# Loading the expert numbers of the tiles into TensorE's registers: eight at a time or two at a time

## The chip, the cores and the metric

The kernel runs on one core of one Trainium2 chip. The metric is device time in microseconds (us) of one execution, the median of several runs. Its engines are named as the profile names them: PE (TensorE, with PEld for its weight loads and PEldq for what its sequencer does itself), DVE (VectorE), ACT (ScalarE), POOL (GpSimd) and SP (SyncE).

## The reference, cut to what matters

The program is a chain of four blocks, each added to its input after a layernorm: differential attention (batch 16, 256 tokens, width 128), a two-layer window-attention transformer, a linear state-space recurrence, and a mixture of experts. Only the last is touched:

```python
xt = x.reshape(-1, D)                        # 4096 tokens, D = 128
logits = xt @ router_w.T                     # 8 experts
topk_vals, topk_idx = jax.lax.top_k(logits, 2)
g = jax.nn.sigmoid(topk_vals)
g = g / (g.sum(axis=-1, keepdims=True) + 1e-10)
out = jnp.zeros_like(xt)
for e in range(E):
    ge = jnp.sum(jnp.where(topk_idx == e, g, jnp.zeros_like(g)), axis=-1)
    h = jax.nn.silu(xt @ w_gate[e]) * (xt @ w_up[e])      # width 256
    out = out + ge[:, None] * (h @ w_down[e])
```

Every token takes part in two experts only, so the kernel sorts the tokens by expert and multiplies each with the weights of its own two.

## The kernel before, in words

A stage called `dispatch` has written every token's row (128 numbers, its place and its expert) into a region of DRAM for each of its two experts. `mixture_of_experts` then works through 72 tiles (`SLOTS = 2 * TILES + NE`) of 128 rows, each of one expert. Which expert a tile has is known only on the chip: VectorE counts (`tiles_of_experts`) and writes the expert of each tile into `c["count"]` and the place of its rows into `c["place"]`, both int32 in SBUF, then raises `listed`.

What each engine does with the tiles, in a fixed order written out by hand as Python loops:

- SyncE loads eight places at a time into registers (L1757) and issues one load per tile into a ring of 16 (`xin`, L1763). A slot is used again once TensorE has turned its rows (`x_full`) and VectorE has aimed them (`aimed`).
- TensorE: `turn_x(q)` transposes the rows of tiles 2q and 2q+1 into `psX` (L1918); `gate_up(i)` multiplies tile i with the gate and up weights of its expert, 512 columns, into `psG` (L1925); `turn_h(i)` transposes the hidden values (L1933); `down(i)` multiplies with the down weights, two halves (L1941). The order in iteration i is: `turn_x` for the next pair (even i), `gate_up(i + 1)`, `turn_h(i)`, `down(i - 1)`.
- ScalarE moves the transposed rows out of PSUM (`mx_xT`, L1873), takes silu of the gate half (`mx_sl`, L1880) and moves the turned hidden values (`mx_hT`, L1886).
- VectorE multiplies silu with the up half (`mx_h`, L1847), copies the result out (`mx_y`, L1854), and every eight tiles works out where rows go (`aim`).
- GpSimd scatters the 128 result rows of each tile to DRAM (`mx_results`, L1772).

The weights of all experts lie in SBUF (`m_experts`). The address of a tile's weights is computed from a register of TensorE's sequencer, which `load_experts(n)` (L1901 to L1907) fills: eight values of `c["count"]` per call (`SHARE = 8`), in one TENSOR_LOAD followed by a FUSED_REGOPS and a SEQ_ASSERT for each value, all recorded under L1903. It is called once ahead of the loop and then at i = 4, 12, ..., 60 for the tiles from i + 4 on, between `turn_x` and `gate_up(i + 1)`. Each product has a further FUSED_REGOPS of its own for the address (recorded under L1925 and L1941), and waits for semaphores that don't fit on an instruction are EVENT_SEMAPHORE instructions of the sequencer (L1931 ahead of `turn_h`, L1939 ahead of `down`).

Behind the last tile and its scatter a barrier follows, and then the stage that fetches both results of each token, weighs and adds them, normalises and stores.

Of the kernel before, what the change touches and what calls it, by code (L numbers as in the profile page):

```python
# [1473 lines left out]
NE = 8  # L1474
# [6 lines left out]
SLOTS = 2 * TILES + NE  # L1481
SHARE = 8
# [217 lines left out]
def mixture_of_experts(nc, X, F, out, rows, results, consts, c, w, pay, top, seen):  # L1700
# [7 lines left out]
    with ExitStack() as ctx:  # L1708
# [4 lines left out]
        with ExitStack() as tiles_ctx:  # L1713
# [35 lines left out]
            def x_of(eng, i):  # L1749
                eng.wait_ge(landed[i % RING], 16 * (i // RING + 1))  # L1750

            @block.sync
            def _(sp):
                sp.wait_ge(listed, 1)
                for i in range(SLOTS):
                    if i % SHARE == 0:
                        _, at = nc.values_load_multi_w_load_instructions(  # L1757
                            c["place"][0:1, i:i + SHARE], engines=(mybir.EngineType.SP,), min_val=0,
                            max_val=(NE + 1) * TILES * P - P)
                    if i >= RING:  # L1760
                        sp.wait_ge(x_full, (i - RING) // 2 + 1)
                        sp.wait_ge(aimed, (i - RING) // SHARE + 1)
                    sp.dma_start(xin[:, i % RING, :], rows[bass.ds(at[i % SHARE], P), :])\  # L1763
                      .then_inc(landed[i % RING], 16)
# [133 lines left out]
            @block.tensor  # L1898
            def _(pe):
                chosen = {}  # L1900

                def load_experts(n):
                    _, values = nc.values_load_multi_w_load_instructions(  # L1903
                        c["count"][0:1, n * SHARE:(n + 1) * SHARE], engines=(mybir.EngineType.PE,), min_val=0,
                        max_val=NE - 1)
                    for k, v in enumerate(values):
                        chosen[n * SHARE + k] = v  # L1907

                def of_expert(i, c0, c1):
                    return weights[:, bass.ds(chosen[i], 1), c0:c1].rearrange("p a n -> p (a n)")  # L1910

                def turn_x(q):
                    for i in (2 * q, 2 * q + 1):
                        x_of(pe, i)
                    if q >= 1:
                        pe.wait_ge(xT_ready, q)
                    for a in range(2):
                        ins = pe.transpose(psX[:, a * P:(a + 1) * P], xin[:, (2 * q + a) % RING, 0:D], ident[:, :])  # L1918
                    ins.then_inc(x_full, 1)

                def gate_up(i):
                    pe.wait_ge(xT_ready, i // 2 + 1)
                    if i >= 2:
                        pe.wait_ge(h_ready, i - 1)
                    pe.matmul(psG[:, i % 2, :], xT[:, i // 2 % 2, i % 2, :], of_expert(i, 0, DOWN), start=True, stop=True)\  # L1925
                      .then_inc(g_full, 1)

                def turn_h(i):
                    pe.wait_ge(h_ready, i + 1)
                    if i >= 2:  # L1930
                        pe.wait_ge(hT_ready, i - 1)  # L1931
                    for j in range(J):
                        ins = pe.transpose(psH[:, i % 2, j * P:(j + 1) * P], h[:, i % 2, j * P:(j + 1) * P], ident[:, :])  # L1933
                    ins.then_inc(t_full, 1)

                def down(i):
                    pe.wait_ge(hT_ready, i + 1)
                    if i >= 2:
                        pe.wait_ge(y_ready, i - 1)  # L1939
                    for j in range(J):  # L1940
                        ins = pe.matmul(psY[:, i % 2, 0:D], hT[:, i % 2, j * P:(j + 1) * P],  # L1941
                                        of_expert(i, DOWN + j * D, DOWN + (j + 1) * D), start=(j == 0), stop=(j == J - 1))
                    ins.then_inc(y_full, 1)

                pe.matmul(psC[:, 0:NE], c["ones"][:, :], seen[:, GROUPS, :], start=True, stop=True).then_inc(counted, 1)
                pe.wait_ge(listed, 1)
                load_experts(0)
                turn_x(0)
                gate_up(0)
                for i in range(SLOTS):  # L1950
                    if i % 2 == 0 and i + 2 < SLOTS:
                        turn_x(i // 2 + 1)
                    if i % SHARE == SHARE // 2 and i // SHARE + 1 < SLOTS // SHARE:
                        load_experts(i // SHARE + 1)
                    if i + 1 < SLOTS:
                        gate_up(i + 1)
                    turn_h(i)
                    if i >= 1:
                        down(i - 1)
                down(SLOTS - 1)  # L1960
# [327 lines left out]
```

## Time and profile before

| what | us |
| --- | --- |
| runs, median (lowest to highest of 3) | 2120.12 (2118.52 to 2121.19) |
| the profiled execution, its own time | 2117.38 |
| span of its records | 2115.6 |
| PE busy in the span | 1730.7 (82%) |
| DVE busy | 1544.2 (73%) |
| ACT busy | 1364.1 (64%) |
| POOL busy | 876.9 (41%) |
| mean granted clock of TensorE (share of full speed) | 0.906 |

The profile is of one execution. Times in its rows are counted from the span's start. A row of the timeline merges like instructions in a row; what stands in brackets is how long the engine was idle before and what released it. "issue" is idle time in which the engine waited for nothing that the profile shows, so it is its sequencer that was late. Register and semaphore instructions do not count as busy; they are found under PEldq at their line. A matmul's end is modelled, so that two matmuls in a row can overlap in the rows. The granted clock (PEclk) is 1.00 for 2.4 GHz and 0.50 for 1.2 GHz, or a mean over both.

### The profile page before, as it was taken

The page shows a single profiled execution, that of the slowest core. Times are in us where ns is not written, and L with a number is a line of the kernel's source. Part 1 is how long each engine was busy: PE and PEld are TensorE (multiplying, and loading weights), DVE is VectorE, ACT ScalarE, POOL GpSimd, SP SyncE. Part 2 cuts the span into 40 slices and gives each one's busy share as a digit, 9 for nine tenths or more (in the row PEclk, how much of TensorE's full clock was granted, in tenths as well). Part 3 has the DMA queues.
Part 4 walks back from the last instruction along what each step waited for, and adds up shares of the span by engine and source line. Part 5 has one row for each costly group of instructions (what it writes and reads, how often), then busy time and mean ns, then how long its engine had stood idle before and what let it go on. Part 6 is the DMA issues. An engine that isn't in the chain of part 4 may idle for free. (4 is left out here: it accounts for less than half of the span.)

```text
span 2115.6 us, 39585 instructions
## 1 busy us (share of the span) xinstructions
PE 1730.7 (82%) x12410; PEld 1135.5 (54%) x12410; DVE 1544.2 (73%) x4156; ACT 1364.1 (64%) x4708; POOL 876.9 (41%) x816
## 2 busy tenths in 40 slices
PE   4999999999999937999996868999996836426881
PEld 2555555555555515777774535777773514424550
DVE  3888999898988857999994658999993656513334
ACT  2888888888888835888883226888882262303444
POOL 3555555565555633333321233323231231662444
PEclk9999999999999957999998979999998966558995
DMA  7990000000000000000001100000001000112214
GB/s 208 202 155 2 2 2 2 2 2 2 2 2 2 2 5 6 17 11 16 16 16 24 27 6 11 11 16 17 16 11 33 18 1 1 36 46 66 64 45 128
DMA packets 102527, 65.92 MB, mean 31 GB/s; under 512 B 27698, under 2 KB 93874, under 8 KB 102322
## 3 DMA queue, kind: packets, MB, share of 16 engines
q1 hardware_dynamic: 97970, 54.40, 12.3%
q0 software_dynamic: 4352, 8.99, 1.2%
q8 instruction: 104, 1.70, 0.3%
q14 instruction: 101, 0.83, 0.1%
HBM read 19.50 MB, written 30.24 MB: 24 GB/s over the span
## 5 line engine op out<-in xcount | busy, mean ns | idle before, releaser
L411 ACT ACTIVATE a_E<-a_psS,a_nm 128x128 f32<-128x128 f32 (+1 forms) x1028 | 419.9, 429 | 31.2 <-DVE a_nm L245 28.8
L216 POOL TENSOR_SCALAR a_aT<-a_dT 128x384 f32<-128x384 f32 x256 | 309.8, 1210 | 298.8 <-PE a_psO L529 187.3
L245 DVE TENSOR_REDUCE a_nm<-a_psS 128x2 f32<-128x256 f32 (+1 forms) x514 | 259.9, 546 | 43.8 <-PE a_psS L496 43.2
L492 PE MATMUL a_psS<-a_kT,a_qm 32*128 32x128 f32 (+1 forms) x2064 | 240.6, 351 | 5.7 <-issue 3.7
L270 DVE SCALAR_TENSOR_TENSOR a_d<-a_E,a_cf 128x128 f32<-128x128 f32 (+1 forms) x512 | 219.5, 469 | 27.9 <-DVE a_cf L259 1.4
L411 ACT ACTIVATION_READ_ACCUMULATOR a_E<-a_psS,a_nm 128x1 f32 x1028 | 220.6, 215 | 0.0
L830 POOL TENSOR_TENSOR b0rn<-b0ss,minus_half 128x16 f32<-128x16 f32 x36 | 107.2, 2977 | 224.2 <-DVE b0ss L866 224.2
L830 POOL TENSOR_TENSOR b1rn<-b1ss,minus_half 128x16 f32<-128x16 f32 x36 | 107.2, 2977 | 223.3 <-DVE b1ss L866 223.3
L420 ACT ACTIVATE a_dT<-a_psT 128x384 f32<-128x384 f32 x256 | 127.0, 496 | 73.8 <-PE a_psT L505 71.1
L492 PEld LDWEIGHTS a_psS<-a_kT,a_qm 32*128 32x128 f32 x2064 | 136.6, 186 | 56.1 <-issue 35.7
L505 PE MATMUL a_psT<-ident,a_d 128*128 128x128 f32 x768 | 132.4, 281 | 6.1 <-DVE a_d L270 0.3
L1772 POOL DMA_INDIRECT mx_results<-mx_y,mx_targetu x72 | 68.8, 955 | 106.3 <-DVE mx_y L1854 105.7
L505 PEld LDWEIGHTS a_psT<-ident,a_d 128*128 128x128 f32 x768 | 87.6, 141 | 34.7 <-DVE a_d L270 28.4
L1847 DVE TENSOR_TENSOR mx_h<-mx_psG,mx_sl 128x256 f32<-128x256 f32 x72 | 30.6, 425 | 102.7 <-ACT mx_sl L1880 99.0
L496 PE MATMUL a_psS<-causal,identb 128*128 128x256 bf16 x516 | 101.8, 279 | 0.0
L1925 PE MATMUL mx_psG<-m_experts,mx_xT 128*128 x144 | 83.9, 668 | 18.7 <-issue 18.1
L964 ACT ACTIVATE b0E<-b0psS,b0nm 128x128 f32<-128x128 f32 x260 | 92.0, 377 | 10.0 <-DVE b0nm L894 10.0
L964 ACT ACTIVATE b1E<-b1psS,b1nm 128x128 f32<-128x128 f32 x260 | 92.0, 377 | 8.7 <-DVE b1nm L894 8.7
L1077 PE MATMUL b0psQ<-wqk,b0hT 128*128 128x512 f32 x148 | 81.3, 676 | 16.9 <-DVE b0part L875 12.0
L1077 PE MATMUL b1psQ<-wqk,b1hT 128*128 128x512 f32 x148 | 80.4, 669 | 16.8 <-DVE b1part L875 11.3
L1046 PEld LDWEIGHTS b0psS<-b0kT,b0qm 128*128 128x128 f32 x528 | 72.1, 198 | 18.2 <-issue 16.3
L518 PE MATMUL a_psO<-a_dT,a_vp 128*32 128x256 f32 x516 | 81.2, 393 | 0.6 <-ACT a_dT L420 0.6
(353 smaller groups left out, 4425.7 us busy)
## 6 DMA issues: line engine op xcount, KB each, us to landing
mx_rows<-mx_blank SPq DMA_DIRECT2D x9, 2080.0 KB, 27.9
mx_xin<-mx_rows SPq DMA_DIRECT2D x72, 65.0 KB, 1.9
b0v<-b0v SPq DMA_DIRECT2D x34, 128.0 KB, 2.3
b1v<-b1v SPq DMA_DIRECT2D x34, 128.0 KB, 2.3
F<-mx_results SPq DMA_DIRECT2D x8, 256.0 KB, 5.1
mx_second<-mx_results SPq DMA_DIRECT2D x8, 256.0 KB, 5.6
out_dram<-X SPq DMA_DIRECT2D x8, 256.0 KB, 2.3
f0z<-F SPq DMA_DIRECT2D x9, 128.0 KB
```

The lines of the kernel that those rows point to most:

```text
L216: pool.tensor_scalar(aT[:, s, :], dT[:, s, :], 0.0, None, ALU.max).then_inc(positived.sem, 1)
L245: ins = dve.tensor_reduce(nm[:, s, t, :], psS[:, s, :, (0, P)[t]:(P, 384)[t]], axis=AX.X, op=ALU.max, negate=True)
L270: ins = dve.scalar_tensor_tensor(out=d[:, s, c0:c1], in0=E[:, s, 1, c0:c1], scalar=cf[:, s, t:t + 1], in1=E[:, s, 0, c0:c1], op0=ALU.mult, ...
L411: ins = act.activation(E[:, s, m, c0:c1], psS[:, s, m, c0:c1], ACT.Exp, bias=nm[:, s, t, m:m + 1], accum_out=Z[:, p, h, t, m:m + 1])
L420: act.activation(dT[:, s, :], psT[:, s, 0:384], ACT.Copy).then_inc(evaced.sem, 1)
L492: pe.matmul(psS[:, s, m, c0:c1], qm[rows, p, a, r, t * P:(t + 1) * P], kT[rows, p, a, 0:c1 - c0], start=(t == 0), stop=False)
L496: ins = pe.matmul(diagonal, identb[:, :], causal[:, :].unsqueeze(1).broadcast_to([P, 2, P]), start=False, stop=True)
L505: ins = pe.transpose(psT[:, s, c * P:(c + 1) * P], d[:, s, c * P:(c + 1) * P], ident[:, :])
L830: pool.tensor_tensor(rn[:, t, :], ss[:, t, :], minus_half[:, 0:2 * H], ALU.pow).then_inc(rn_ready.sem, 1)
L964: ins = act.activation(E[:, s, n, :], psS[:, s, n * P:(n + 1) * P], ACT.Exp, bias=nm[:, s, n:n + 1], accum_out=Z[:, s, n:n + 1])
L1077: ins = pe.matmul(psQ[:, n * W:(n + 1) * W], hT[:, p, t * P:(t + 1) * P], wqk[:, n * W:(n + 1) * W], start=True, stop=True)
L1925: pe.matmul(psG[:, i % 2, :], xT[:, i // 2 % 2, i % 2, :], of_expert(i, 0, DOWN), start=True, stop=True)\
```

## The change

`load_experts` takes two values a call instead of eight. The first call, ahead of the loop, is for tiles 0 and 1; then it is called at every even i for tiles i + 2 and i + 3. Its place in the iteration is now behind `gate_up(i + 1)`, ahead of `turn_h(i)`, where it stood between `turn_x` and `gate_up(i + 1)`. Nothing else is changed. TensorE's stream gets 36 TENSOR_LOADs in place of 9, and the same 72 pairs of register instructions. All lines behind L1904 are one lower in the changed kernel between the two edits.

```diff
-                def load_experts(n):
+                def load_experts(i):
                     _, values = nc.values_load_multi_w_load_instructions(
-                        c["count"][0:1, n * SHARE:(n + 1) * SHARE], engines=(mybir.EngineType.PE,), min_val=0,
-                        max_val=NE - 1)
+                        c["count"][0:1, i:i + 2], engines=(mybir.EngineType.PE,), min_val=0, max_val=NE - 1)
                     for k, v in enumerate(values):
-                        chosen[n * SHARE + k] = v
+                        chosen[i + k] = v
...
                 for i in range(SLOTS):
                     if i % 2 == 0 and i + 2 < SLOTS:
                         turn_x(i // 2 + 1)
-                    if i % SHARE == SHARE // 2 and i // SHARE + 1 < SLOTS // SHARE:
-                        load_experts(i // SHARE + 1)
                     if i + 1 < SLOTS:
                         gate_up(i + 1)
+                    if i % 2 == 0 and i + 2 < SLOTS:
+                        load_experts(i + 2)
                     turn_h(i)
                     if i >= 1:
                         down(i - 1)
```

On TensorE, iteration 4 before: the turns of x for tiles 6 and 7, the load for tiles 8 to 15 (`ISA x16` are the eight register pairs), and the gate-and-up product of tile 5.

```order
L1941 MATMUL mx_psY<-m_experts,mx_hT 128x128
L1918 MATMUL mx_psX<-ident,mx_xin 128x128 x2
L1903 TENSOR_LOAD mx_count
L1903 ISA x16
L1925 ISA
L1925 MATMUL mx_psG<-m_experts,mx_xT 128x512
```

The same iteration on TensorE in the changed kernel, up to the first down product of tile 3.

```order
L1940 MATMUL mx_psY<-m_experts,mx_hT 128x128
L1917 MATMUL mx_psX<-ident,mx_xin 128x128 x2
L1924 ISA
L1924 MATMUL mx_psG<-m_experts,mx_xT 128x512
L1903 TENSOR_LOAD mx_count
L1903 ISA x4
L1932 MATMUL mx_psH<-ident,mx_h 128x128 x2
L1940 ISA
L1940 MATMUL mx_psY<-m_experts,mx_hT 128x128
```

The product of tile 5 has moved ahead of the load, the load has four register instructions instead of sixteen, and it stands in front of the turns of h of tile 4. The same piece comes in each even iteration.

## Rows read from the trace of the kernel before

**Rows 1.** The page's head
```profile
span 2115.6 us, 39585 instructions
```

**Rows 2.** Busy time by stretches of the expert tiles (columns in its first line)
```profile
core 0: us, PE busy (x) PEld busy (x) DVE busy (x) ACT busy (x) POOL busy (x), PEclk, DMA share, GB/s
1912.00:2072.00 160.00, 135.29 (x648) 88.22 (x648) 50.47 (x171) 63.62 (x181) 68.78 (x72) 0.89 0.22 61
...
1928.50:1932.00 3.50, 3.41 (x9) 2.24 (x10) 0.45 (x2) 0.77 (x2) 0.00 (x0) 0.53 0.50 128
1932.00:1943.00 11.00, 11.00 (x62) 7.34 (x60) 4.50 (x16) 5.46 (x17) 6.30 (x7) 1.00 0.27 73
1945.80:1958.70 12.90, 12.90 (x70) 8.68 (x71) 4.86 (x18) 6.18 (x19) 6.36 (x7) 1.00 0.23 62
1961.30:1966.00 4.70, 4.70 (x16) 3.03 (x17) 1.12 (x3) 1.43 (x4) 0.96 (x1) 0.64 0.07 20
```

**Rows 3.** Waits of PE, 1912 to 2072 us (total us, times, longest)
```profile
PE mx_psG L1925 <- issue: 18.1, 8, 2.4
PE mx_psX L1918 <- DMA mx_xin<-mx_rows: 10.9, 1, 10.9
```

**Rows 4.** Timeline of PE (start, us, engine, line, op, operands, times)
```profile
1925.82 0.38 PE L1918 MATMUL mx_psX<-ident,mx_xin 128*128 128x128 f32 x2
1928.59 2.07 PE L1925 MATMUL mx_psG<-m_experts,mx_xT 128*128 x2 [2.39 <-issue]
...
1936.57 0.38 PE L1918 MATMUL mx_psX<-ident,mx_xin 128*128 128x128 f32 x2
1936.79 1.02 PE L1925 MATMUL mx_psG<-m_experts,mx_xT 128*128 x2
...
1943.11 0.38 PE L1918 MATMUL mx_psX<-ident,mx_xin 128*128 128x128 f32 x2
1945.79 1.12 PE L1925 MATMUL mx_psG<-m_experts,mx_xT 128*128 x2 [2.30 <-issue]
...
2062.22 0.38 PE L1918 MATMUL mx_psX<-ident,mx_xin 128*128 128x128 f32 x2
```

**Rows 5.** Line 1903, all nine loads (ns min/median/max, first and last start)
```profile
L1903 PEldq FUSED_REGOPS  x72: 146/146/165, 1910.2 to 2047.1; - x72
L1903 PEldq SEQ_ASSERT  x72: 18/18/28, 1910.4 to 2047.3; - x72
L1903 PEldq TENSOR_LOAD <-mx_count x9: 587/591/778, 1909.3 to 2044.3; - x9
```

**Rows 6.** Line 1903 from 1925 to 1929 us, the second load
```profile
L1903 PEldq FUSED_REGOPS  x8: 146/146/151, 1926.0 to 1928.1; - x8
...
L1903 PEldq TENSOR_LOAD <-mx_count x1: 611/611/611, 1925.4 to 1925.4; - x1
```

**Rows 7.** Line 1931 from 1951.5 to 1952.5 us, ahead of the turns of h
```profile
L1931 PEldq EVENT_SEMAPHORE  x1: 51/51/51, 1951.8 to 1951.8; - x1
```

**Rows 8.** Line 1939 from 1951.5 to 1953.4 us, ahead of the down product
```profile
L1939 PEldq EVENT_SEMAPHORE  x1: 51/51/51, 1952.6 to 1952.6; - x1
```

**Rows 9.** Timeline of all engines, 1952.1 to 1953.5 us, an undisturbed pair
```profile
1952.16 0.42 DVE L1847 TENSOR_TENSOR mx_h<-mx_psG,mx_sl 128x256 f32<-128x256 f32 x1 [0.91 <-ACT mx_sl L1880]
...
1952.42 1.02 PE L1925 MATMUL mx_psG<-m_experts,mx_xT 128*128 x2
...
1953.29 0.38 PE L1933 MATMUL mx_psH<-ident,mx_h 128*128 128x128 f32 x2
1953.29 0.14 PEld L1933 LDWEIGHTS mx_psH<-ident,mx_h 128*128 128x128 f32 x1 [0.29 <-issue]
1953.40 0.41 PEld L1941 LDWEIGHTS mx_psY<-m_experts,mx_hT 128*128 128x128 f32 x3
```

**Rows 10.** Timeline of POOL, the last two scatters
```profile
2069.13 0.96 POOL L1772 DMA_INDIRECT mx_results<-mx_y,mx_targetu  x1 [0.30 <-issue]
2070.39 0.95 POOL L1772 DMA_INDIRECT mx_results<-mx_y,mx_targetu  x1 [0.30 <-issue]
```

**Rows 11.** Timeline of SP's queue, 1912 to 1923.7 us
```profile
1912.35 11.38 SPq L1763 DMA_DIRECT2D mx_xin<-mx_rows  x16
```

## The prediction

> **What bounds the kernel now.** The change touches one stage, so the first question is where that stage lies and how much of the execution it is. The span is 2115.6 us [rows 1]. The 72 expert tiles run between 1912 and 2072 us, and only that stretch can change; the merge behind it waits for its last scatter and moves along with it. The second view is the busy time by stretches [rows 2]. Between 1932 and 1943 us TensorE is busy 11.00 of 11.00 us at a granted clock of 1.00, while VectorE has 4.50, ScalarE 5.46 and GpSimd 6.30: inside a batch of eight tiles TensorE alone bounds the stage. Over the whole stage it is busy only 135.29 of 160.00 us, at a mean clock of 0.89. The third view, who waited for whom, says where the rest goes [rows 3]: 10.9 us once for the first rows to land, and 18.1 us in 8 waits, 2.4 at most, ahead of a gate-and-up product, released by "issue". That is not another engine but TensorE's own sequencer.
>
> The timeline shows the places [rows 4]. The two turns of x at 1943.11 are followed by a product only at 1945.79, where the normal distance is 0.22 (1936.57 to 1936.79). The records of line 1903 say what the sequencer does meanwhile [rows 5]: each load of eight registers is one TENSOR_LOAD of 0.59 us and then eight pairs of FUSED_REGOPS (0.146) and SEQ_ASSERT (0.018). For the load of tiles 8 to 15 the first record starts at 1925.4 and the last pair at about 1928.2 [rows 6], so it takes 2.9 us; 0.61 of that is the TENSOR_LOAD and 2.3/8 = 0.29 is one pair with its gap. The product resumes at 1928.59.
>
> The same rows say something that the forecast needs: the load started at 1925.4, yet the turns of x that stand ahead of it in the program began on the array at 1925.82 [rows 4, 6]. So the load did not wait for the array to be empty; the sequencer runs ahead, and only what exceeds its lead (2.9 less the idle 2.4) becomes a hole.
>
> The hole is not the whole loss. After it the clock falls: 0.53 over the 3.50 us from 1928.50 and 0.64 over the 4.70 us from 1961.30 [rows 2], which is 3.3 and 3.4 us at 1.2 instead of 2.4 GHz, and costs half of that, 1.7 us. After the hole at 1943.11 it did not fall (1.00 from 1945.80 on).
>
> **The change, part by part.**
>
> *Removed: eight loads of eight inside the stage.* I price this by what the stage would take without any hole. The turns of x for pair 3 start at 1925.82, those of pair 35 at 2062.22 [rows 4]: 32 pairs in 136.40 us. Undisturbed, 1936.57 to 1943.11 are two pairs, 3.27 us each, and 32 x 3.27 = 104.6 us. The difference is **31.8 us**. It splits as 18.1 us idle, 8 x 0.16 = 1.3 us in which the turns' modelled end (0.38) covers what is really idle beyond 0.22, and 12.4 us of slow clock, about seven drops of 1.7 us. The clock part comes back only if no new holes make it fall.
>
> *The first load (8 to 2 values).* It ends 6 x 0.29 = 1.7 us earlier, but TensorE then waits for the first rows anyway (10.9 us) [rows 3]. Nothing.
>
> *Added: 35 loads of two, behind the product of tile i+1 (i even), ahead of the turns of h.* The number of register pairs stays at 72; 27 TENSOR_LOADs come on top. One such load takes 0.59 + 2 x 0.29 = 1.17 us, with the gap behind TENSOR_LOAD 1.2 us of the sequencer. What covers it is seen in an undisturbed pair. The sequencer reaches the semaphore instruction of the turns of h at 1951.8 [rows 7], having passed the product already, while the array starts that product at 1952.42 and the turns of h at 1953.29 [rows 9]. Its next record is at 1952.6 [rows 8]: for 0.8 us it stood at the weight load of h, which waits for VectorE's h, ready at 1952.16 + 0.42 = 1952.58 [rows 9]. So 0.8 us of the 1.2 lie in a wait that exists anyway, and the other 0.4 come out of the lead. The semaphore instruction now starts at 1951.8 + 1.2 = 1953.0, and the weight load about 0.1 behind it, at 1953.1; the array wants to go on at 1953.29, and weight load to matmul takes about 0.1 when chained (the second weight load of the turns starts at 1953.29, the next product's first at 1953.40). That leaves **0.0 to 0.1 us of margin**. The instructions of the down product follow as fast as the array takes them, and at the turns of h of the odd tile, where no load stands, the sequencer waits for h again and has its lead back for the next pair. So a late pair is not carried on as a growing delay.
>
> How long a TENSOR_LOAD of two takes, no row shows. From below it is bounded by a share of the row in proportion, 0.59 x 2/8 = 0.15 us; from above by the longest of the nine, 0.78 us [rows 5]. I take 0.59, the typical row, since the value is most likely a fixed trip. With 0.15 the margin is 0.5 us; with 0.78 the turns of h come 0.1 us late in each of the 33 pairs from tile 4 on, 3.3 us in all. A shorter load gains nothing, because TensorE is full anyway. The Trainium skill (Runtime: NRT & Kernel Launch, Instruction fetch mechanics) gives about 200 ns per register for such loads; that would be 1.6 us for eight, where the trace has 0.59, so the measurement decides. By that page two registers would take 0.4 us, and the sum would stay the same with 0.2 us more margin.
>
> *Other queues.* GpSimd's scatters can follow each other at 1.27 us (2069.13 to 2070.39) [rows 10], against 1.63 us per tile. SyncE issued 16 row loads with one register load of its own among them in 11.4 us, 0.7 us per tile [rows 11]. The seven-tile stretches between the holes run at the new pace already, without a wait for either. Nothing here becomes the bound.
>
> *Sum.* Minus 31.8, plus 0.3 for a few pairs that come late: minus 31.5 us. The profiled execution takes 2117.38 us and would take 2085.9; it lies 2.7 us below the median of the runs, 2120.12, so the median becomes **2088.6 us**. That is 1.5% less; about 0.2%, 4 us, is what a measurement of this kernel can tell from no change.
>
> **The rivals.**
>
> 1. *Short holes, and a clock that keeps falling.* If the margin of 0.0 to 0.1 is missed by 0.2 us per pair, 33 x 0.2 = 6.6 us are lost, and if the clock then falls as often as now, seven times, the 12.4 us stay lost too: a gain of 12.8, **2107 us**. For it speaks how thin the margin is; against it, that the present holes are 2.3 us long and one of the eight left the clock alone. The Trainium skill (TensorE: Matmul & The Clock Gate, A second HAM failure mode: psum-queue depth-cycling) describes just this, frequent micro-idles of TensorE that make its clock oscillate; no row here shows it inside an undisturbed batch. Chance 0.09.
> 2. *The slow clock is not the holes' doing.* The drops follow the holes closely, but one hole had none. If they stay for a reason that is not issue, 12.4 us are not recovered: 31.8 - 12.4 = 19.4, **2100.7 us**. Against it, every stretch measured at 1.00 is free of holes. Chance 0.08.
> 3. *The load waits behind the product until the array is idle (slower).* Then nothing hides it: 1.2 us in each of 33 pairs, 39.6 us, against 19.4 us of holes removed, with the clock's loss kept: **2140 us**. It decides from 19.4/33 = 0.6 us of idle time per pair on. For it: the load stands at a new place, behind the longest matmuls of the stage. Against it: the nearest rows, where the load began 0.4 us before the turns ahead of it [rows 4, 6]. Chance 0.05.
> 4. *No effect.* The holes move but their sum stays, since the register pairs are as many as before: 72 x 0.29 = 21 us of sequencer time either way. This would need the wait for h to stop hiding them; 1 us of idle per pair makes it so (31.8/33). **2120 us**, chance 0.02.
>
> **How the numbers follow.** The forecast has the remaining 0.76. Its own spread is 2086 to 2093: the median moves by 1 us either way in the runs shown, and the long load adds 3.3 us. The range of 2085 to 2102 takes in rival 2 and leaves out rivals 1, 3 and 4 and what is mis-sized, 2 in 10. Rivals 1 and 2 are both faster by over 0.2%, so faster is 0.93; the same 0.02; slower 0.05.
>
> **What the profile after would show.** 36 TENSOR_LOADs on TensorE's sequencer; the wait for "issue" ahead of the gate-and-up products, 18.1 us now, gone or under 1 us; the turns of x 3.27 to 3.3 us apart from pair 3 to pair 35; a granted clock of 1.00 over the stage once it is up (0.95 or so over the stage instead of 0.89); the stage ending near 2040 instead of 2072 us. New idle time ahead of the turns of h would be the margin missed (rival 1 if the clock falls with it). A clock below 1.00 in a stretch without holes would be rival 2. TENSOR_LOADs that start only when the product has ended would be rival 3. The forecast is wrong if the pair takes over 3.4 us at full clock, or if GpSimd or SyncE appear as what TensorE waits for.

## The result, and the profile after

| | us |
| --- | --- |
| changed kernel, median of 4 runs | 2090.89 (2088.86 to 2092.62) |
| before, median of the 4 runs beside it | 2119.43 (2118.52 to 2121.19) |
| ratio | 0.9864 (95% interval 0.9847 to 0.9881) |
| the profiled execution, its own time | 2092.62 (before 2117.38) |

The change made the kernel 28.5 us faster; 31.5 was forecast, and the interval of the ratio is 25.2 to 32.4 us. The page's head and TensorE's waits over the expert tiles answer to [rows 1, 3]:

```profile
span 2090.8 us, 39546 instructions
```
```profile
PE mx_psX L1917 <- DMA mx_xin<-mx_rows: 11.0, 1, 11.0
PE mx_psG L1924 <- ACT mx_xT L1873: 0.6, 1, 0.6
PE mx_psH L1932 <- issue: 0.3, 1, 0.3
```

The 18.1 us behind "issue" are gone; the wait for the first rows is as it was. Busy time by stretches, from pair 3 to pair 35, beside the same stretch of the kernel before (columns as in [rows 2]):

```profile
1932.50:2037.70 105.20, 105.20 (x578) 70.68 (x577) 44.09 (x153) 54.38 (x161) 61.18 (x65) 1.00 0.28 77
```
```profile
1926.00:2062.00 136.00, 117.90 (x575) 77.55 (x574) 44.61 (x152) 54.91 (x160) 60.73 (x65) 0.91 0.21 60
```

TensorE is busy 105.20 of 105.20 us at a granted clock of 1.00. The first and the last turns of x of that stretch, and two ordinary pairs, in its timeline:

```profile
1932.43 0.38 PE L1917 MATMUL mx_psX<-ident,mx_xin 128*128 128x128 f32 x2
...
1935.70 0.38 PE L1917 MATMUL mx_psX<-ident,mx_xin 128*128 128x128 f32 x2
...
1938.97 0.38 PE L1917 MATMUL mx_psX<-ident,mx_xin 128*128 128x128 f32 x2
...
2037.65 0.38 PE L1917 MATMUL mx_psX<-ident,mx_xin 128*128 128x128 f32 x2
```

32 pairs take 105.22 us where they took 136.40 [rows 4]: **31.2 us less**, with 3.27 us a pair. The loads themselves, answering to [rows 5]:

```profile
L1903 PEldq FUSED_REGOPS  x72: 151/151/165, 1917.6 to 2038.2; - x72
L1903 PEldq SEQ_ASSERT  x72: 18/18/28, 1917.8 to 2038.4; - x72
L1903 PEldq TENSOR_LOAD <-mx_count x36: 532/537/722, 1916.8 to 2037.3; - x36
```

The two profiled executions differ by only 24.8 us, mainly because this one reached the expert tiles 7.5 us later: the first load is at 1916.8, and was at 1909.3 [rows 5]. No instruction ahead of the tiles was changed, and the delay is already there in the stage before: GpSimd's last scatter of `dispatch` starts at 1902.8 instead of 1895.3. Experiment e5 looks at this.

### The profile page after: what moved, and what is told of

It is laid out like the page before. It is cut to its first block and busy times, and to the rows that moved or that the text cites. A ratio compares the mean times of both kernels' runs of the same rounds, so it can differ in the third digit from the quotient of the medians.

```text
span 2090.8 us, 39546 instructions
## 1 busy us (share of the span) xinstructions
PE 1710.1 (82%) x12344; PEld 1127.9 (54%) x12410; DVE 1544.7 (74%) x4156; ACT 1361.3 (65%) x4708; POOL 875.8 (42%) x816
## 5 line engine op out<-in xcount | busy, mean ns | idle before, releaser
L1077 PE MATMUL b0psQ<-wqk,b0hT 128*128 128x512 f32 x148 | 80.3, 668 | 16.9 <-DVE b0part L875 11.9
L527 PE MATMUL a_psO<-a_aT,a_twos 128*32 128x256 f32 x516 | 81.2, 393 | 0.5 <-POOL a_aT L216 0.5
L1046 PEld LDWEIGHTS b1psS<-b1kT,b1qm 128*128 128x128 f32 x528 | 71.7, 197 | 18.2 <-issue 16.3
## 6 DMA issues: line engine op xcount, KB each, us to landing
mx_rows<-mx_blank SPq DMA_DIRECT2D x9, 2080.0 KB, 31.8
```

The lines of the kernel that those rows point to most:

```text
L1077: ins = pe.matmul(psQ[:, n * W:(n + 1) * W], hT[:, p, t * P:(t + 1) * P], wqk[:, n * W:(n + 1) * W], start=True, stop=True)
```

## The experiments

All times below are medians; they were taken on several chips, and the kernel before took 2119.4 us beside the changed kernel, 2116.2 beside e1 to e4, 2116.3 beside e5 to e8 and 2116.5 beside e9 to e11, which ran once each. So the ratios can be compared between groups, and the times only within one. "Pairs 3 to 35" is the time from the turns of x of pair 3 to those of pair 35, "hole" what a pair takes beyond 3.27 us when the cost of the slow clock is left out, and a "drop" a stretch at a granted clock of 0.50 between those two pairs.

| kernel | time, us | ratio to before | pairs 3 to 35, us | hole, us | drops of the clock |
| --- | --- | --- | --- | --- | --- |
| before | 2119.4 | 1 | 136.40 | 8 x 2.5 | 7 |
| changed | 2090.9 | 0.9864 | 105.22 | none | 0 |
| e1 eight, behind the product | 2098.9 | 0.992 (0.990 to 0.994) | 118.96 | 8 x 1.8 | 0 |
| e2 two, at the old place | 2108.2 | 0.9961 (0.9947 to 0.9974) | 126.84 | 32 x 0.7 | 0 |
| e3 no loads | 2084.5 | 0.9858 (0.9840 to 0.9877) | 104.64 | none | 0 |
| e4 each load twice | 2110.8 | 0.9979 (0.9970 to 0.9989) | 130.10 | 32 x 0.8 | 0 |
| e5 changed, again | 2087.1 | 0.9859 (0.9843 to 0.9876) | 105.12 | none | 0 |
| e6 two, odd iterations | 2085.7 | 0.9862 (0.9846 to 0.9879) | 104.64 | none | 0 |
| e7 six, old place | 2119.6 | 1.0011 (1.0001 to 1.0020) | 134.15 | 2.1 and 2.8 in turn | 3 |
| e8 twelve, behind | 2107.6 | 0.9962 (0.9948 to 0.9976) | 128.17 | 5 x 3.0 | 4, one twice as long |
| e9 eight and one, behind | 2118.9 | one run | 135.59 | 8 x 2.4 | 7 |
| e10 no loads, short holes at the old place | 2094.8 | one run | 117.06 | 8 x 1.6 | 0 |
| e11 before, again | 2115.0 | one run | 136.46 | 8 x 2.5 | 7 |

**e1 and e2: the place alone, the size alone.**

```diff
-                    if i % SHARE == SHARE // 2 and i // SHARE + 1 < SLOTS // SHARE:
-                        load_experts(i // SHARE + 1)
                     if i + 1 < SLOTS:
                         gate_up(i + 1)
+                    if i % SHARE == SHARE // 2 and i // SHARE + 1 < SLOTS // SHARE:
+                        load_experts(i // SHARE + 1)
                     turn_h(i)
```

> Eight values at a time as before, but behind the gate-and-up product of the same iterations (i = 4, 12, ...). Theory (the load is paid only beyond TensorE's sequencer wait for h and its lead): a load of eight takes 2.9 us and has 0.8 + 0.4 us of cover at this place, so a hole of about 1.7 us remains ahead of the turns of h, eight times, where 2.3 us stood ahead of the product; the clock still falls behind most. Time 2110 to 2116 us, some 5 us under before. Rival (the place alone hides a load, the size hardly matters): no hole over 0.3 us, 2090 to 2095 us.

The hole is as expected, and stands where it was expected; TensorE's timeline at the load for tiles 16 to 23:

```profile
1942.68 0.38 PE L1918 MATMUL mx_psX<-ident,mx_xin 128*128 128x128 f32 x2
1942.90 1.02 PE L1925 MATMUL mx_psG<-m_experts,mx_xT 128*128 x2
1945.49 0.41 PE L1933 MATMUL mx_psH<-ident,mx_h 128*128 128x128 f32 x2 [1.57 <-DVE mx_h L1847]
...
1947.80 0.38 PE L1918 MATMUL mx_psX<-ident,mx_xin 128*128 128x128 f32 x2
```

This pair takes 5.12 us, 1.85 more than 3.27. The releaser named is VectorE, whose h had long been ready; it is the sequencer that was late. What was not expected is the clock: it never fell, and so the time of 2098.9 us lies 11 us under the range of 2110 to 2116.

```profile
1928.00:2047.00 119.00, 106.95 (x579) 70.51 (x578) 44.69 (x153) 55.32 (x160) 61.33 (x65) 1.00 0.25 68
```

So the place alone is worth 17.4 us of the 31.2 (136.40 - 118.96): 5.5 in shorter holes, and the 11.9 that seven drops of 3.41 us cost (half of their length, as between 1.2 and 2.4 GHz). e2 is the other half; its loop calls `load_experts(i + 2)` at each even i, between `turn_x` and `gate_up(i + 1)`.

> Two values at a time, but at the old place, between the turns of x and the gate-and-up product. Theory: the 1.1 us of the load come behind the sequencer's wait for h and ahead of the product, so only the lead of about 0.6 to 0.7 us covers them; the product comes 0.4 to 0.5 us late in each of 33 pairs, 13 to 17 us, ahead of any loss of clock. Time 2103 to 2112 us; if the short holes make the clock fall as the 2.3 us holes did, up to 2125. Rival (size alone does it): 33 pairs at 3.27 us, 2090 us.

```profile
1943.67 0.38 PE L1917 MATMUL mx_psX<-ident,mx_xin 128*128 128x128 f32 x2
1944.44 1.12 PE L1924 MATMUL mx_psG<-m_experts,mx_xT 128*128 x2 [0.39 <-DVE mx_h L1847]
...
1947.59 0.38 PE L1917 MATMUL mx_psX<-ident,mx_xin 128*128 128x128 f32 x2
```

A pair of 3.92 us: 0.65 late, 0.69 in the mean over 32, where 0.4 to 0.5 were expected. From the start of such a load to the sequencer's next instruction 1.17 us pass in most pairs, so the lead of the sequencer at the old place is 0.5 us (1.17 - 0.69), and not the 0.6 to 0.7 that were assumed. Neither half alone does what both do: the size makes the load short enough, the place gives it the wait for h as cover.

**e3 and e4: no load, and twice as much.** e3 takes the load out of the loop and indexes the registers with `chosen[i % SHARE]`; e4 calls `load_experts(i + 2)` twice.

> Only the first load of eight; all tiles take their weights' addresses from these eight registers, so tiles 8 to 71 are multiplied with the weights of other experts than theirs. No load in the loop. Theory: this is the floor of the stage, 3.27 us per pair from pair 3 to pair 35 (104.6 us; 105.2 in the changed kernel), so the time is within 1 us of the changed kernel, 2088 to 2091 us, at a clock of 1.00 over the stage. Rival (the loads still cost something that the timeline does not show as idle, or other engines are now the bound): over 3 us below the changed kernel, or pairs that stay above 3.27 us.

> The changed kernel with each load of two issued twice. Theory: 2.1 us of sequencer per pair where 1.1 to 1.2 are covered, so the turns of h come about 0.9 us late in each of 33 pairs: 30 us at full clock, 2120 us; if the clock falls as well, 2130 to 2150 us. Rival (TensorE has enough work queued to hide any load behind a product): under 2 us more than the changed kernel.

Every pair of e3 takes 3.27 us, from these turns of x to those, and TensorE is never idle:

```profile
1923.55 0.38 PE L1918 MATMUL mx_psX<-ident,mx_xin 128*128 128x128 f32 x2
...
2028.19 0.38 PE L1918 MATMUL mx_psX<-ident,mx_xin 128*128 128x128 f32 x2
```
```profile
1924.00:2028.00 104.00, 104.00 (x573) 70.28 (x572) 43.41 (x151) 53.99 (x159) 60.50 (x64) 1.00 0.28 78
```

104.64 us in all is the floor of the stage, and the changed kernel stands 0.6 us above it. The time of e3, 2084.5 us, lies below its range and over 3 us below the 2090.9 of the changed kernel, as its rival has it. Half of that is the chips: the kernel before is 3.2 us faster there. By the ratios (0.9858 against 0.9864, and 0.9859 in e5) the two kernels can't be told apart, and no pair is above 3.27 us. In e4 the turns of h are late in each pair; its waits:

```profile
PE mx_psH L1932 <- issue: 17.5, 34, 0.6
```

0.80 us per pair beyond the floor, where 0.9 were expected. The two loads keep the sequencer for 2.4 us (from 1944.9 to the semaphore instruction at 1947.4 in one pair), so 1.6 us are covered. In e1 it was 1.2 us: the load takes 3.0 us and leaves a hole of 1.8. The cover is thus no constant of the place. In e4 the sequencer starts its loads 0.8 us ahead of the turns of x (1944.9 against 1945.71), in e1 and in the changed kernel 0.4 us (1942.3 against 1942.68 in e1). Why it is further ahead there is not shown. The clock stayed at 1.00 in both e2 and e4, with a short hole in every pair.

**e5 and e6: the changed kernel again, and a place with more cover.** e6 loads behind the product of the odd iterations:

```diff
-                    if i % 2 == 0 and i + 2 < SLOTS:
-                        load_experts(i + 2)
+                    if i % 2 == 1 and i + 3 < SLOTS:
+                        load_experts(i + 3)
```

with one more `load_experts(2)` ahead of the loop.

> The changed kernel once more, to see what of the difference outside the expert tiles (its first profile reached them 7.5 us later than the kernel before) is its own. Theory (chance of the run): the expert tiles begin between 1907 and 1912 us of the span as in the other five kernels, pair 3 to pair 35 takes 105.2 us again, and the time is 1.3 to 1.5% under before. Rival (the change slows the dispatch stage ahead of it): the tiles begin at 1916 us or later again.

> Two values at a time behind the gate-and-up product of the odd iterations (where no turns of x stand), for tiles i + 3 and i + 4, and tiles 2 and 3 loaded ahead of the loop. The sequencer waits about 1.06 us for h there instead of 0.74. Theory: the load of 1.1 us is hidden with 0.3 us more margin, so no pair is late: 3.27 us in every one, 104.6 to 104.7 us from pair 3 to pair 35, 0.5 us under the changed kernel, not to be told from it by the times. Rival (late pairs come from something else than the thin margin): 105.0 us or more, with pairs of 3.3 to 3.4 us.

e5 has its first load at 1911.3, as late as the latest of the others apart from the first profile of the change (1905.3 in e6 to 1911.3), and 105.12 us for the pairs: the late start of the first profile is not the change's doing, as far as two profiles tell. e6 has 3.27 us in every pair, exactly e3's 104.64: the 0.6 us of the changed kernel are its thin cover. By the times the two can't be told apart (0.9862 and 0.9859), so e6 is at best 0.5 us better.

**e7 to e11: what makes the clock fall.** After e1 two theories were left: the length of a hole, or its place. e7 loads six at the old place, e8 twelve behind the product (i = 8, 20, ...).

> Six values at a time at the old place, between the turns of x and the product (i = 2, 8, ...), 11 loads in the loop. The load takes 0.59 + 6 x 0.29 = 2.3 us, so with the same lead as before the hole is 1.7 us, ahead of the product as before. Theory (the length of the hole decides on the clock): as in the kernel with eight values behind the product, whose holes were 1.75 us, the clock stays at 1.00 from pair 3 on; 11 x 1.7 = 19 us of holes, 2104 to 2107 us against 2088 without. Rival (the place decides: holes ahead of the product make the clock fall): drops of 3.4 us behind most holes, 16 us more, 2118 to 2124 us.

> Twelve values at a time behind the product (i = 8, 20, ...), 5 loads in the loop. The load takes 0.59 + 12 x 0.29 = 4.0 us, of which 1.2 are covered, so holes of 2.8 to 2.9 us stand ahead of the turns of h. Theory (length decides): the clock falls behind most of the five, 1.7 us each; 5 x 2.85 + about 4 x 1.7 = 21 us over the floor, 2106 to 2110 us. Rival (place decides, behind the product it never falls): 14 us over the floor, 2101 to 2103 us, clock 1.00 from pair 3 on.

e7 did not tell the two apart, though its time of 2119.6 us lies in the range of the rival, because a load of six costs something else than expected:

```profile
L1903 PEldq TENSOR_LOAD <-mx_count x12: 815/1242/1524, 1911.0 to 2051.1; - x12
```

They alternate between 0.82 us (first value at a multiple of twelve) and 1.47 to 1.52 us (at an odd multiple of six). The holes were so 2.1 and 2.8 us instead of 1.7, and the clock fell behind 3 of 10: behind two of five long ones and one of five short ones. So the excess over the floor is longer holes in the main (24.4 of 29.5 us), and not the drops of the rival. e8 refutes that the clock never falls behind the product: it falls behind 4 of the 5 holes of 3.0 us, once for 6.8 us instead of 3.4. e9 adds to e1 one load of a single value, e10 adds to e3 two loads of two values, unused, at the old place of i = 4, 12, ...:

```diff
+                        nc.values_load_multi_w_load_instructions(
+                            c["count"][0:1, 0:1], engines=(mybir.EngineType.PE,), min_val=0, max_val=NE - 1)
```

> Eight values at a time behind the product, as in e1, and behind each a further load of one value that nothing uses. The load becomes 2.93 + 0.54 + 0.29 = 3.8 us; the hole ahead of the turns of h grows from 1.8 us to 2.6 us, the pair to 5.9 us, as long as a pair with a hole and full clock in the kernel before (5.83). Theory (the length of the hole decides whether the clock falls): drops of 3.4 us behind most of the eight holes, pairs of 7 us and more, about 2112 us. Rival (behind the product the clock never falls): 1.00 from pair 3 on, eight pairs of 5.9 us, about 2105 us.

> As e3 (no loads in the loop, tiles 8 to 71 multiplied with the weights of other experts), with two loads of two values that nothing uses at the old place in i = 4, 12, ... They take 2 x 1.15 = 2.3 us, of which some 0.4 are covered, so eight holes of 1.8 to 1.9 us stand ahead of the product. Theory (length decides): the clock stays at 1.00 from pair 3 on, eight pairs of 5.1 us, about 15 us over e3, 2098 to 2100 us. Rival (place decides: ahead of the product the clock falls): drops behind most holes, 2108 us or more.

> The kernel before once more, to see whether its seven drops of the clock behind eight holes repeat. Theory: six to eight drops of 3.4 us again, eight pairs of 5.8 or 7.3 to 7.6 us, 136 us from pair 3 to pair 35. Rival (the drops are a chance of the one run): 0 to 4 of them and 125 to 130 us.

e9 against e1 is the clean pair: same place, same eight values, only the hole is longer.

```profile
1943.87 1.02 PE L1925 MATMUL mx_psG<-m_experts,mx_xT 128*128 x2
1947.11 0.41 PE L1933 MATMUL mx_psH<-ident,mx_h 128*128 128x128 f32 x2 [2.21 <-issue]
1947.35 1.01 PE L1941 MATMUL mx_psY<-m_experts,mx_hT 128*128 x4
1948.15 1.92 PE L1925 MATMUL mx_psG<-m_experts,mx_xT 128*128 x2
```
```profile
1928.50:2064.00 135.50, 118.38 (x577) 77.65 (x576) 45.28 (x153) 55.99 (x160) 61.29 (x64) 0.91 0.21 60
```

The product behind the hole takes 1.92 instead of 1.02 us, and the granted clock over the stretch is 0.91 as before the change, 1.00 in e1. e10 has holes of 1.6 us at the old place, where 1.8 to 1.9 were expected, and a clock of 1.00:

```profile
1923.00:2040.00 117.00, 106.52 (x577) 71.29 (x578) 43.91 (x153) 54.40 (x160) 61.28 (x64) 1.00 0.25 69
```

e11 repeats the kernel before to 0.06 us over the 32 pairs, seven drops included; the hole without one is now the first, and was the second. With one hole in every fourth pair it is then the length that matters, and not the place: no drop behind 16 holes of 1.4 to 2.0 us (e1 and e10), but behind 7 of 8 of about 2.3 to 2.6 us in each of three executions (before, e11 and e9). It isn't length alone. The hole that goes free is no shorter than the others (2.6 us in the kernel before), and of e7's holes, one in every third pair, one of 2.1 us made the clock fall while three of 2.8 us did not. How often the holes come and at what moment they fall was not varied by itself, so what else counts stays open.

## Why the prediction was right, point by point

- *The holes and their clock, minus 31.8 us.* Right: without any load in the loop (e3) the same 32 pairs take 104.64 us, 31.8 less than the 136.40. The changed kernel has 31.2 of it, and the other 0.6 is what its own loads cost. That both parts come back together was right, too: rival 2 (the clock is not the holes' doing, chance 0.08) fell with e9 against e1.
- *The added loads are hidden.* Right: "issue" ahead of the products is gone. Rival 3 (a load waits until the array is idle) fell too. In the changed kernel this load starts at 1948.5, ahead of the turns of x (1948.87) and the product (1949.09) that stand before it:

```profile
L1903 PEldq TENSOR_LOAD <-mx_count x1: 538/538/538, 1948.5 to 1948.5; - x1
```
```profile
1948.87 0.38 PE L1917 MATMUL mx_psX<-ident,mx_xin 128*128 128x128 f32 x2
...
1949.09 1.02 PE L1924 MATMUL mx_psG<-m_experts,mx_xT 128*128 x2
1949.70 0.38 PEld L1932 LDWEIGHTS mx_psH<-ident,mx_h 128*128 128x128 f32 x2 [0.42 <-issue]
1949.95 0.38 PE L1932 MATMUL mx_psH<-ident,mx_h 128*128 128x128 f32 x2
```

- *A margin of 0.0 to 0.1 us at the turns of h.* Too small for an ordinary pair: the weights of h are loaded at 1949.70, 0.25 us before their matmul, and where they come late the matmul follows after 0.05 (1979.39 and 1979.44 below), so the margin is 0.2 us. The load of two took 0.537 and not the 0.59 that I took, and the step from weight load to matmul is 0.05 and not 0.1. What I had passed over is the instruction behind: "the instructions of the down product follow as fast as the array takes them" failed. A late pair, in TensorE's timeline and at line 1940:

```profile
1979.39 0.20 PEld L1932 LDWEIGHTS mx_psH<-ident,mx_h 128*128 128x128 f32 x2 [0.62 <-DVE mx_h L1847]
1979.44 0.39 PE L1932 MATMUL mx_psH<-ident,mx_h 128*128 128x128 f32 x2
...
1979.73 0.71 PE L1940 MATMUL mx_psY<-m_experts,mx_hT 128*128 x4
```
```profile
L1940 PEldq FUSED_REGOPS  x2: 51/51/51, 1979.6 to 1979.7; - x2
```

  The turns of h are on time, but the down product starts 0.29 behind them instead of 0.22 and lasts 0.71 instead of 0.61, because its two address computations come at 1979.6 and 1979.7, when the array is already there. Six of the 32 pairs are late in this way, the down product lasting 0.65 to 0.71 us: by 0.04 to 0.17 us, 0.57 us in all; 0.3 was in the sum. What uses up the margin in five of them is a delay of the sequencer itself. It starts the load only 0.2 to 0.3 us ahead of the turns of x instead of about 0.4 (three pairs, this one among them: 1978.1 against 1978.36), or takes 1.34 us for it instead of 1.17 (two pairs). What delays it is not shown. With the load behind the product of the odd iterations (e6) no pair is late.
- *Late pairs don't add up.* Right: the pair behind a late one takes 3.27 again.
- *Rival 1 (short holes make the clock fall, 0.09).* It did not come up, and e2 and e4 show that it would not have even with the margin missed: 32 holes of 0.7 to 0.8 us in each, with a clock of 1.00. The failure mode that the Trainium skill describes (TensorE: Matmul & The Clock Gate, A second HAM failure mode: psum-queue depth-cycling), frequent micro-idles that make the clock oscillate, was not seen here for holes of that length.
- *The total.* 31.5 forecast against 28.5 (25.2 to 32.4) and, in e5, 29.2 (26.2 to 33.2). Both intervals hold the stage's 31.2, so the times alone would not have told 31.2 from 28; the stage's own figure rests on the profiles. What lies between is outside the tiles, whose first load came between 1905.3 and 1916.8 us in thirteen profiles; whether the change has a share in it is open.

## What to carry to other kernels

A sequencer that runs ahead of its array hides its own work up to its lead plus any semaphore wait that it stands in anyway (here 0.4 and 0.8 us); look for that wait (two consecutive sequencer records far apart), put the register loads in front of it, and cut them to its length. Judge such a move against the undisturbed period of the loop and not by idle time alone, since here a hole of 2.5 us mostly cost 1.7 us more in slow clock, and one of 1.8 us nothing. The odd iterations had more cover here: between two places choose the one whose existing wait is longer.

## What the runs showed of the hardware that was not expected

- A register load does not cost in proportion to its count: one value took 0.31 us (right behind a load of eight), two 0.537, eight 0.591, twelve 0.85, and six 0.82 or 1.47 us by where they begin. The first load of an execution took longer (0.72 to 0.79 us for two or eight). Here is the load of one value in e9:

```profile
L1957 PEldq TENSOR_LOAD <-mx_count x8: 304/309/312, 1930.7 to 2049.2; - x8
```

  The register pairs behind the values (0.29 us each) take longer than the load itself in all of them but the load of one. The Trainium skill (Runtime: NRT & Kernel Launch, Instruction fetch mechanics) gives about 200 ns per register, with an eye to the loads that the runtime injects around a kernel; by that figure eight would take 1.6 us, and this kernel's own load of eight took 0.59.
- In e4, the second of two loads in a row took 0.54 to 0.68 us, the same load alone 0.54.
- Holes of 0.7 to 0.8 us in every pair, or of 1.6 to 1.8 us in every fourth, left TensorE's clock at 2.4 GHz; behind holes of 2.4 to 2.5 us in every fourth it fell to 1.2 GHz seven times out of eight, each time for 3.4 us.
